# A grouped-edge attention stage on one core: TensorE adds a tile's eight slots and its carry in one run

## The reference

```
w_m = (efeat @ W_msg + b_msg).reshape(E, in_f, -1)
w_a = (efeat @ W_attn + b_attn).reshape(E, in_f, -1)
h_src = feat[src][:, :, None]
e1 = w_m * h_src
e2 = w_a * h_src
seg_max = jax.ops.segment_max(e2, dst, num_segments=N)
ex = jnp.exp(e2 - seg_max[dst])
denom = jax.ops.segment_sum(ex, dst, num_segments=N)
attn = ex / denom[dst]
ft = jax.ops.segment_sum(e1 * attn, dst, num_segments=N)
return ft.sum(axis=1)
```

## Time and profile before

| What | Value |
|---|---|
| Median of 3 runs | 6362.89 us |
| Profiled execution, its time | 6367.98 us |
| Its span | 6365.9 us |
| Mean granted TensorE clock | 0.883 of full speed |
| DVE busy, share of the span | 5234.9 us, 82% |
| POOL busy | 4810.0 us, 76% |
| PE busy | 4660.5 us, 73% |
| ACT busy | 2605.3 us, 41% |

### The profile page before, as it was taken

One profiled execution on the slowest core, in us unless ns is written; L12 is line 12 of the kernel. 1 busy time (PEld: TensorE's weight loads), 2 busy tenths in 40 slices (PEclk: granted clock), 3 DMA queues, 4 the chain that ended last, 5 costly groups with the idle time before them and its releaser, 6 DMA issues. The chain is left out here.

```text
span 6365.9 us, 70880 instructions
## 1 busy us (share of the span) xinstructions
PE 4660.5 (73%) x18115; PEld 2234.1 (35%) x18115; DVE 5234.9 (82%) x8985; ACT 2605.3 (41%) x4586; POOL 4810.0 (76%) x4137
## 2 busy tenths in 40 slices
PE   1177777777777777776888888888888888888881
PEld 1133333333333333333333333333333333333330
DVE  5366666666666666667999999999999999999996
ACT  1122222222222222222555555555555555555553
POOL 6688888888888888873777777777777777777772
PEclk6588888888888988898999999999999999999995
DMA  4122222222222222220111111111111111111112
GB/s 124 48 79 79 78 79 78 79 78 78 83 64 64 64 65 64 64 63 18 26 27 27 27 25 27 27 27 26 26 27 27 27 25 27 27 27 25 27 23 106
DMA packets 394268, 316.42 MB, mean 50 GB/s; under 512 B 243117, under 2 KB 334678, under 8 KB 393985
## 3 DMA queue, kind: packets, MB, share of 16 engines
q0 software_dynamic: 233920, 200.74, 14.2%
q1 hardware_dynamic: 160318, 115.35, 6.0%
HBM read 220.37 MB, written 168.56 MB: 61 GB/s over the span
## 5 line engine op out<-in xcount | busy, mean ns | idle before, releaser
L618 POOL DMA_INDIRECT bg<-btab,mt x1600 | 2119.5, 1325 | 492.4 <-issue 487.5
L979 POOL DMA_INDIRECT xg<-x1tab,edge x1920 | 1975.7, 1029 | 585.2 <-issue 584.3
L746 PE MATMUL pagg<-ohh,stt 125*128 125x512 bf16 x4800 | 1854.1, 422 | 749.8 <-DVE ohh L669 749.8
L1050 PE MATMUL ps<-work,ident 128*128 128x512 f32 x3840 | 1945.8, 631 | 0.2 <-DVE work L1138 0.2
L747 PE MATMUL pagg<-ohh,stt 125*128 125x270 bf16 x4800 | 1458.8, 304 | 0.0
L1099 DVE TENSOR_TENSOR work<-pw,xg 128x1024 f32<-128x1024 f32 x960 | 1113.0, 1212 | 21.5 <-DMA xg<-x1tab,edge 21.5
L1039 PE MATMUL pw<-w,et 99*128 99x512 bf16 x1920 | 682.2, 442 | 570.4 <-DVE work L1099 564.6
L746 PEld LDWEIGHTS pagg<-ohh,stt 125*128 125x128 bf16 x4800 | 512.0, 107 | 1506.3 <-DVE ohh L669 828.2
L1050 PEld LDWEIGHTS ps<-work,ident 128*128 128x128 f32 x3840 | 781.8, 204 | 726.6 <-issue 634.5
L651 DVE TENSOR_TENSOR bg<-bg,e 125x1024 f32<-125x1024 f32 x200 | 245.2, 1226 | 849.8 <-DMA bg<-btab,mt 849.8
L1022 ACT ACTIVATE work<-work,mt 128x256 f32<-128x256 f32 x1920 | 861.4, 500 | 131.6 <-DVE work L1099 109.0
(11 more groups left out here) (231 smaller groups left out, 3932.9 us busy)
## 6 DMA issues: line engine op xcount, KB each, us to landing
etab<-joined SPq DMA_DIRECT2D x200, 199.2 KB
xg<-x1tab,edge POOLq DMA_INDIRECT x1920, 2.3
bg<-btab,mt POOLq DMA_INDIRECT x1600, 3.4
rtab<-zrow SPq DMA_DIRECT2D x56, 384.0 KB, 5.6
tab<-rtab SPq DMA_DIRECT2D x7, 2048.0 KB, 8.3
e<-in_edge_attr_dram SPq DMA_DIRECT2D x200, 62.5 KB
e<-in_edge_attr_dram SPq DMA_DIRECT2D x200, 31.2 KB
mt<-meta SPq DMA_DIRECT2D x240, 6.0 KB
```

The costliest lines, as they stand in the source:

```text
L618: g.indirect_dma_start(bg[:, h, i, :], None, btab, bass.IndirectOffsetOnAxis(ap=mt[:, h, 0, i:i + 1], axis=0)).then_inc(gathered[h], 16)
L746: pe.matmul(pagg[:, 0, :], w, ohh[:, h, i, 0:CUT], start=False, stop=False, skip_group_check=True)
L979: g.indirect_dma_start(xg[:, b % 4, i, :], None, x1tab, bass.IndirectOffsetOnAxis(ap=edge[:, b, i, EW - 1:EW], axis=0)).then_inc(x_in[b % ...
L1050: pe.matmul(ps[:, b % 2, :], ident[:, :], work[:, b % 4, i, :, :, :].rearrange("p i a o -> p (i a o)"), start=i == 0, stop=False)
```

## The change

Only TensorE's order in the stage's body is changed; its instructions and their number are the same. All eight totals of `done` and its carry are now issued in one run, with the eight transposes of `next_but_one` between the sixth and the seventh total. Behind the carry follow the eight weighings: slots 4 to 7 of `ahead` and then slots 0 to 3 of `next_but_one`, whose one wait for the copy of the transposed records stands ahead of its four weighings. No other engine's list changes.

```diff
                     if done:
-                        for i in range(J - 3):
+                        for i in range(J - 2):
                             total(done, i)
                     if next_but_one:
...
                         for i in range(J):
                             ins = pe.transpose(pt[0:KS, b % 2, i, :], edge[:, b, i, 0:EW - 1].bitcast(BF16)[:, 0:KS], identb[:, :])
                         ins.then_inc(turned, 1)
-                    if ahead:
-                        for i in range(4, J):
-                            weigh(ahead, i)
-                    if done:
-                        total(done, J - 3)
-
-                    if next_but_one:
-                        pe.wait_ge(et_copied, next_but_one[0] + 1)
-                        for i in range(2):
-                            weigh(next_but_one, i)
                     if done:
                         total(done, J - 2)
-                    if next_but_one:
-                        for i in range(2, 4):
-                            weigh(next_but_one, i)
-                    if done:
                         total(done, J - 1)
                         n, b, r = done
                         pe.wait_ge(carried, n + 1)
                         pe.matmul(ps[:, b % 2, :], ident[:, :], carry[:, b % 2, :], start=False, stop=True).then_inc(summed, 1)
+                    if ahead:
+                        for i in range(4, J):
+                            weigh(ahead, i)
+                    if next_but_one:
+                        pe.wait_ge(et_copied, next_but_one[0] + 1)
+                        for i in range(4):
+                            weigh(next_but_one, i)
```

## The result

The changed kernel takes 6577.98 us (median of 4 runs, 6574.23 to 6583.42) against 6362.33 us of the kernel before beside it: ratio 1.0338, 95% interval 1.0325 to 1.0351. That is 216 us more, where I had forecast 168 us more and a range of 6385 to 6660 us. The profiled execution has a span of 6575.7 us, 209.8 us above the one before.

A forecast was written before the change was run, and what follows sets the result against it. DVE was taken to bound the stage; 120 half-clock stretches at 1.45 us each, 174 us, less 6 us of today's loss gave +168 us, 6536 us against the profiled execution and 6531 us for the median, range 6385 to 6660 us.

The forecast's parts named there:

- What bounds the stage: Changed stage: DVE, busy 99%, sets the time at 13.525 us a tile; the change can win at most 6 us.
- Where the clock falls: PE's clock falls while only four weighing pairs run, so half clock then lies on the run of totals.
- The case in which the clock holds: Rival: without a pause above 0.9 us PE stays at 2.4 GHz, DVE never waits; 6357 us, chance 0.13.
- How often: Half-clock stretches come in about every second tile, as after the kernel before's empty 2.6 us pause: 120 stretches.
- The thin stretch: PE from 7.7 to 12.6 us in a tile: 4.9 us with only four weighing pairs, 1.8 us of work.
- What one costs: Half clock for 4.3 us takes 2.15 us from PE; less 0.45 and 0.25, DVE waits 1.45 us.
- the slack: Room before DVE waits for its third L1099: weighings ready at 8.4, wanted at 8.85, so 0.45 us.
- my chain: PE's full-clock sequence: twelve matmuls from -0.9 to 4.25, transposes, load to 5.05, four more to 6.75, carry ending 7.7.
- The 6 us that I gave back: DVE's loss in the kernel before, 240 x (13.525 - 13.50) = 6 us, subtracted from the forecast's 174 us.
- Short stalls: Rival: clock falls every second tile but mostly misses the totals; 0.3 us a time, +30 us, 6393 us, chance 0.20.
- Every tile: Rival: half clock in each tile, since a late run delays the next wait; 240 x 1.3 = 312 us, 6669 us, chance 0.15.
- What was moved for others: Sums out at 7.7 instead of 16.4, so ACT's L1026 no longer waits, POOL's scatter is served sooner: 0 us.

The follow-up runs named there:

- the filled old order: Kernel before with ten unread matmuls behind the transposes, which keep one PSUM bank: 6336.9 us, kernel before 6368.1, one run each.
- the kernel of six orders: The changed kernel's stage loop split into six loops, each with its own TensorE order, transposes in one bank: 6402.4 us, kernel before 6360.8.
- the filled order: Changed kernel with two unread matmuls behind each pair of weighings, transposes in one bank: 7214.2, 7215.6, 7230.9, 7220.7 us on disturbed chips.
- the kernel with the carry behind: Changed kernel with the carry's matmul moved behind the weighings of slots 4 to 7: 7203.9, 7202.1, 7237.5 us on disturbed chips; second run 7202.1.

## Why the prediction was right, and where its sizes were not

*What bounds the stage.* Right. DVE is paced by its own instructions where nobody is late, and all that was lost went through one wait of DVE's. It was worth looking for how much half a clock costs the order before, 0.09 us in a tile that it hits, since this showed what the order protects. The trace bears it out: 77 of 230 tiles take over 13.55 us.

*Where the clock falls.* Right in kind: no idle time above 0.9 us, and yet it falls, and it is low over the run of totals. The case in which the clock holds had 0.13. The Trainium skill, "TensorE: Matmul & The Clock Gate", section "HAM oscillation — how this bites in real kernels", names long idle gaps; by that rule the clock would have held, and the trace does not agree. The same page, section "A second HAM failure mode: psum-queue depth-cycling", tells of small idle bits between groups of matmuls that bring the clock down, and with that the trace agrees: 0.53 to 0.89 us of idle time between the pairs, and 174 slow stretches in 194 tiles.

*How often.* Too low. I took one stretch in two tiles from the old pause. The thin stretch is 4.9 us long instead of 2.7, and DVE waits in 174 of 194 tiles, 0.90. The old order's own frequency was read rightly (97 slow stretches in 207 tiles from 3400 to 6200 us), but it was carried over from an empty pause to a longer stretch with four pairs of matmuls in it, and no row said that it would hold there. Why it comes to 0.9 stays open.

*What one costs.* Too high: I had 1.45 us, measured are 170.6 / 174 = 0.98. The stretch itself was sized well. I had 4.3 us, 2.15 lost and 0.25 of that ahead of the run, so 1.90 us on the run; measured are 4.26 us and, in the tiles with a wait, a run that takes 1.96 us longer on average. The mistake sits in the slack, where I had 0.45 us. The changed kernel's tiles bear 3.04 us of extra time to the transposes (8.29 against 5.25 us) for a wait of 2.07, and 1.70 us for 0.73: in both 0.97 us is free. Two terms of my chain were wrong by 0.52 us together. The four totals behind the transposes start 0.45 us after these, not 0.8, and the first total at -1.07, not -0.9. (I also wrote 8.4 where 7.7 and 0.6 make 8.3; the run to the transposes is 0.1 us longer than I had, so the two cancel.) So at full clock the carry's matmul is ready 0.3 us before DVE's L1139 ends, and waits for it (4535.70 above); this wait swallows the first 0.3 us of lateness.

*The sum.* 120 x 1.45 = 174 us was 211.5 us by the page of the profile: 0.9 of 240 tiles are 216, and 0.98 us each. A frequency too low by 0.56 and a price too high by 1.48 nearly cancel; that the forecast is nearer than its terms are is luck. The 6 us that I gave back were less than a clock at full speed brings: tiles without a wait take 13.46 us, not 13.50.

*The other rivals.* Short stalls, 0.3 us a time, are not what is seen; the shortest waits are 0.42 us. "Every tile" had the frequency nearly right, at 1.3 us a tile. What I held against it, that a late PE has fewer thin stretches, did not help much. The timeline suggests why: PE is late in its run only, and DVE still starts the last two pairs of weighings (the pairs at 4554.71 and 4555.84 above). This is argued, not shown.

*What was moved for others.* As forecast, ACT's wait for the sums went and nobody gained by it. L1103 waits for the masks once, 1.0 us ahead of the first tile, as L1110 did before, and never after that.

## What to carry to other kernels

Before a stream of urgent short work and a stream of patient long work are put in separate runs, ask what the clock does in the thin stretch and which work it then hits. In a full engine the urgent pieces belong ahead of the patient ones: here a slow stretch then cost at most 0.09 us instead of 1 us. And TensorE can lose its clock in a stretch without a long pause: here it did so behind pairs of matmuls with 0.53 to 0.89 us of idle time between them. A few matmuls that nobody reads held the clock, at no cost to DVE, because PE had the room.

## What the runs showed of the hardware that was not expected

*The same DVE instructions take 13.41, 13.46 or 13.50 us a tile.* With the clock held and no wait, the filled old order took 13.41 us a tile alone on one chip and 13.50 in the kernel of six orders on another, and the changed one 13.46. The timelines show these differences between the filled old order on its own (first) and in the kernel of six orders (second): the four subtractions take 2.49 against 2.53 us, the four products 2.49 against 2.52, and POOL's long gather starts 0.57 us ahead of the carry in one and 0.07 us behind its start in the other.

```profile
4505.61 2.49 DVE L1136 TENSOR_TENSOR work<-work,state 128x512 f32<-128x512 f32 x4
4508.02 0.69 DVE L1153 TENSOR_TENSOR carry<-state,corr 128x512 f32<-128x512 f32 x1
```
```profile
4507.45 1.47 POOL L980 DMA_INDIRECT xg<-x1tab,edge  x1 [0.30 <-issue]
```
```profile
5311.53 2.53 DVE L1167 TENSOR_TENSOR work<-work,state 128x512 f32<-128x512 f32 x4
5313.98 0.68 DVE L1184 TENSOR_TENSOR carry<-state,corr 128x512 f32<-128x512 f32 x1
```
```profile
5314.05 1.46 POOL L980 DMA_INDIRECT xg<-x1tab,edge  x1 [0.30 <-issue]
```

In the traces most subtractions and products start 0.60 us after the one before, and some 0.65. From 3400 to 6200 us the old order has 1.9 of the longer ones a tile, the changed order 1.0 and the filled old order on its own one in 208 tiles; at 0.045 us each that makes the steps from 13.41 to 13.46 and 13.50 us. What lengthens them is not shown. It goes with where POOL's gathers start: in 400 of the 590 longer ones of the first two a gather or scatter of POOL's begins, but one also begins in 820 of the 2617 others.

The Trainium skill, "GPSIMD Engine Reference", section "1. Specifications", says that POOL shares its SBUF interfaces with VectorE, with contention when a DVE instruction has two SBUF inputs, as these have. The rows are in keeping with it; no run here moves POOL against DVE, so it is argued and not shown. It would be the reason why the filled old order, the fastest version here, gained 31 us and not 6, and why that gain may not be there in every execution: in the kernel of six orders its tiles took 13.50 us, no less than those of the old order around it.

*Late signals of PE.* On the four disturbed chips the stage's tiles mostly alternate between about 13.5 to 14.5 us and 19.5 to 22 us; in two of the four runs of the filled order most take 16 to 18 us. In the kernel with the carry behind (second run) PE has done its transposes at 4514.8 and four weighings by 4519.6, but ACT, which waits for the transposes, and DVE, which waits for the weighings, both go on at 4525.6:

```profile
4514.16 0.61 PE L1062 MATMUL pt<-identb,edge 128*99 128x128 bf16 x8
4514.60 1.94 PE L1050 MATMUL ps<-work,ident 128*128 128x512 f32 x4
4517.84 0.60 PE L1039 MATMUL pw<-w,et 99*128 99x512 bf16 x2 [1.29 <-DVE work L1093]
4518.97 0.60 PE L1039 MATMUL pw<-w,et 99*128 99x512 bf16 x2 [0.53 <-issue]
```
```profile
4525.56 1.01 ACT L1014 COPY et<-pt 99x1024 bf16<-99x1024 bf16 x1 [8.42 <-remote]
```
```profile
4525.58 2.35 DVE L1093 TENSOR_TENSOR work<-pw,xg 128x1024 f32<-128x1024 f32 x2 [6.67 <-remote]
```

"Remote" stands where no instruction of the profile is the releaser. In the trace the six updates of PE's semaphores that were due between 4514.8 and 4520.8 lie between 4525.46 and 4525.67. Nothing of it is seen in the first 2900 us, which are nearly the same in all traces (PE is busy 1923 to 1932 us, the clock is 0.86 or 0.87). Why they are held, and why on some chips only, stays open. It meets every order, so it decides nothing here; it does mean that a kernel has to be compared with its neighbour on the same chip, and that even then 700 us of another cause can cover 200 us of the one under study.
